# One fewer pick matmul per group, group rows in two halves, and scan flags in one PSUM buffer

## What is computed

```
def rgcn_conv(x, src, dst, edge_type, W, root, bias):      # second network, two layers (r0, r1)
    x_src = x[src]
    msg = sum over r of where(edge_type == r, x_src @ W[r], 0)
    norm = 1 / max(count of (dst, edge_type), 1)
    return segment_sum(msg * norm, dst) + x @ root + bias

def _nnconv(x, src, dst, edge_attr, ew, eb, rw, rb):       # fourth network, three layers (c0, c1, c2)
    W = (edge_attr @ ew + eb).reshape(E, 16, 16)
    msg = einsum('ei,eio->eo', x[src], W)
    return segment_sum(msg, dst) + x @ rw + rb
```

## Time and profile before

| | us |
|---|---|
| median of the runs | 12,188.94 |
| the profiled execution, its own time | 12,082.95 |
| its span, first to last instruction | 12,081.0 |
| TensorE matmuls busy | 9,816.9 |
| VectorE busy | 9,313.9 |
| ScalarE busy | 8,267.0 |
| GpSimd busy | 7,589.7 |

### The profile page before, as it was taken

One profiled execution on the slowest core, in us unless ns is written; L12 is line 12 of the kernel. 1 busy time (PEld: TensorE's weight loads), 2 busy tenths in 40 slices (PEclk: granted clock), 3 DMA queues, 4 the chain that ended last, 5 costly groups with the idle time before them and its releaser, 6 DMA issues. The chain is left out here.

```text
span 12081.0 us, 167867 instructions
## 1 busy us (share of the span) xinstructions
PE 9816.9 (81%) x42305; PEld 6821.8 (56%) x42305; DVE 9313.9 (77%) x14722; ACT 8267.0 (68%) x16314; POOL 7589.7 (63%) x6233
## 2 busy tenths in 40 slices
PE   5888888888885079878997688888899689969996
PEld 2333333333332057766775578777777577757775
DVE  7999999999997877764554699997666567656665
ACT  4777777777775057755775488885677467746774
POOL 4555555555556368876776677773677567756775
PEclk7666666666666589988998799998999799979997
DMA  3444444444444267765775111111888578858884
GB/s 117 178 178 177 176 177 178 178 178 178 178 176 138 91 244 269 260 229 188 249 248 167 50 46 44 45 45 26 276 287 290 182 260 293 284 183 268 287 289 161
DMA packets 750362, 2256.05 MB, mean 187 GB/s; under 512 B 272537, under 2 KB 420654, under 8 KB 673806
## 3 DMA queue, kind: packets, MB, share of 16 engines
q10 hardware_dynamic: 161280, 1027.68, 24.1%
q1 hardware_dynamic: 388638, 984.49, 21.7%
q0 software_dynamic: 200304, 242.20, 9.0%
HBM read 1321.84 MB, written 931.93 MB: 187 GB/s over the span
## 5 line engine op out<-in xcount | busy, mean ns | idle before, releaser
L592 POOL DMA_INDIRECT h<-in_x,idx x1568 | 2022.0, 1290 | 1731.9 <-DMA efT<-in_edge_attr_t 1269.9
L676 ACT ACTIVATE PX<-PX,h 128x16 f32<-128x16 f32 x12544 | 2510.5, 293 | 10.2 <-issue 3.8
L625 PE MATMUL PS<-M,minus_ident 128*128 128x512 f32 x1568 | 1417.5, 1030 | 313.9 <-DVE M L710 313.4
L1997 PE MATMUL PS<-mhr,lhs 128*128 128x392 f32 x6272 | 1262.6, 357 | 197.2 <-DVE lhs L2161 171.4
L1479 PE MATMUL PS<-every_weight,dstf 112*128 112x144 f32 (+1 forms) x8960 | 1273.8, 285 | 161.5 <-DVE dstf L1611 114.3
L1479 PEld LDWEIGHTS PS<-every_weight,dstf 112*128 112x128 f32 x8960 | 1223.3, 192 | 317.3 <-DVE dstf L1611 145.3
L1964 POOL DMA_INDIRECT myg<-node_table,mix x784 | 1103.7, 1408 | 447.7 <-issue 230.7
L2060 ACT ACTIVATE mhr<-mhb 128x1568 fp32r<-128x1568 bf16 x784 | 1142.1, 1505 | 294.6 <-DVE mhb L2151 239.0
L1997 PEld LDWEIGHTS PS<-mhr,lhs 128*128 128x128 f32 x6272 | 1152.5, 194 | 282.1 <-ACT mhr L2060 143.8
L613 PE MATMUL PS<-waug,efT 17*128 17x256 f32 x6272 | 1042.3, 535 | 300.0 <-DVE e L688 257.5
L613 PEld LDWEIGHTS PS<-waug,efT 17*128 17x128 f32 x6272 | 612.8, 252 | 1034.4 <-issue 495.6
(11 more groups left out here) (419 smaller groups left out, 20434.1 us busy)
## 6 DMA issues: line engine op xcount, KB each, us to landing
softmax_maxima<-M SPq DMA_DIRECT2D x196, 1024.0 KB
softmax_denominators<-ST SPq DMA_DIRECT2D x196, 1024.0 KB
softmax_numerators<-ST SPq DMA_DIRECT2D x196, 1024.0 KB
one_hot_rows_of_sources<-r0hb ACTq DMA_DIRECT2D x224, 896.0 KB
r1hb<-one_hot_rows_of_sources ACTq DMA_DIRECT2D x224, 896.0 KB
c0hb<-one_hot_rows_of_sources ACTq DMA_DIRECT2D x224, 896.0 KB
c1hb<-one_hot_rows_of_sources ACTq DMA_DIRECT2D x224, 896.0 KB
c2hb<-one_hot_rows_of_sources ACTq DMA_DIRECT2D x224, 896.0 KB
```

The costliest lines, as they stand in the source:

```text
L592: PO.indirect_dma_start(h[b.k][:, at(q), :], None, io["x"], bass.IndirectOffsetOnAxis(ap=idx[b.k][:, q:q + 1], axis=0))\
L625: mm = PE.matmul(PS[0:CH, 4 + n, :], minus[:, :], M[b.k % 2][:, n::4, :], start=False, stop=True)
L676: act = S.activation(PX[b.k][:, 1, t, D * i:D * i + D], PX[b.k][:, 0, t, D * i:D * i + D], ACT.Copy, scale=h[b.k][:, t, i:i + 1])
L1997: mm = PE.matmul(PS[:, 6 + k, 0:A7 // 2], lhs[(G * b.k + q) % 2][:, 2 * two + r, part, :], hr[(2 * G * b.k + j) % 4][:, r, k * A7 // 2:(k ...
```

## The change

It makes these edits:

- The nodes are split in 8 groups of 768 (`A8`, `KB` = 6 slices of 128 places) and a rest of 128 nodes, which counts as a seventh slice of group 0 (high part) and group 4 (low part). A group of edges takes 12 picks of 128 stationary columns and one of 80 columns (`last_parts`): 13.
- The group number is kept twice, once for partitions 0 to 63 and once for 64 to 127: `pick_a` has two halves, and the load of `ra` reads both, each broadcast to 64 partitions. The set-up computes, transposes and stores three arrays in place of two.
- Mask and weighing run over 128 partitions in place of 112.
- The flags `kp` of the scan lie in PSUM banks 2 and 3, one buffer for both blocks, and ScalarE waits for the scan of the block before in place of the second before.

```diff
-A9, KT = 7, 7
+A8, KB, KT = 8, 6, 7
+ROWS = 128 * KB
...
-        pick_a = dram("pick_a", (T, 128), I16)
-        pick_b = dram("pick_b", (T, 128), I16)
+        pick_a = dram("pick_group", (2, T, 128), I16)
+        pick_b = dram("pick_place", (T, 128), I16)
...
-            for n, d_ in enumerate((pick_a, pick_b)):
+            for n, d_ in enumerate((pick_a[0, :, :], pick_a[1, :, :], pick_b)):
...
-            V.tensor_scalar(pab[0][:, :], pab[1][:, :], float(128 * KT), None, ALU.is_ge).then_inc(*vd.up())
-            for k in range(2, A9):
+            V.tensor_scalar(pab[0][:, :], pab[2][:, :], float(ROWS), None, ALU.is_ge).then_inc(*vd.up())
+            V.tensor_scalar(pab[1][:, :], pab[2][:, :], float(A8 * ROWS), None, ALU.is_ge).then_inc(*vd.up())
+            for k in range(2, A8):
...
-            V.scalar_tensor_tensor(out=pab[1][:, :], in0=pab[0][:, :], scalar=-128.0 * KT, in1=pab[1][:, :],
+            V.scalar_tensor_tensor(out=pab[2][:, :], in0=pab[0][:, :], scalar=-float(ROWS), in1=pab[2][:, :],
+                                   op0=ALU.mult, op1=ALU.add).then_inc(*vd.up())
+            V.wait_ge(*vd.now())
+            V.scalar_tensor_tensor(out=pab[0][:, :], in0=pab[1][:, :], scalar=-float(A8 - 1), in1=pab[0][:, :],
+                                   op0=ALU.mult, op1=ALU.add).then_inc(*vd.up())
+            V.wait_ge(*vd.now())
+            V.scalar_tensor_tensor(out=pab[1][:, :], in0=pab[1][:, :], scalar=float(A8 // 2), in1=pab[0][:, :],
                                    op0=ALU.mult, op1=ALU.add).then_inc(*v2t.up())
             V.wait_ge(*pT_up.now())
-            V.wait_ge(*t2v.next(2 * NT))
+            turned_of = t2v.taken
             for k in range(NT):
-                for n in TWO:
+                for n in range(3):
+                    if 3 * k + n in (0, 32):
+                        V.wait_ge(t2v.sem, turned_of + min(3 * k + n + 32, 3 * NT))
                     V.tensor_copy(pT[0:wd[k], k, n, 0:CH], spread_at(k, n)).then_inc(*pT_up.up())
...
+            if c == KB:
+                big_, src_ = tn[:, A8 * KB, :], x[:, A8 * KB, :]
+                V.tensor_copy(last_parts[:, 0:D], big_).then_inc(*vd.up())
+                V.tensor_tensor(last_parts[:, 64:64 + D], src_, big_, ALU.subtract).then_inc(*vd.up())
+                return
...
+        PICKS = 2 * KB + 1
+        LOWEST = 6
...
-                    kp.append(sb(f"{name}kp{k}", [CH, D, TBC], F32, L))
+                    kp.append(PS[0:CH, 2:4, :].rearrange("p b c -> p (b c)")[:, 0:D * TBC].rearrange("p (f t) -> p f t", f=D))
...
-            mx = [dstf[0:A9 * D, 512 * k:512 * k + 512] for k in range(1 + LAG)]
+            mx = [dstf[:, 512 * k:512 * k + 512] for k in range(1 + LAG)]
...
-                SP.dma_start(ra[half][:, :], rows(b, half, pick_a)).then_inc(h_ra[half].sem, 16)
+                groups_of = pick_a[:, some(b, NG + 16 * half, 16), :].rearrange("h t c -> h (t c)")
+                SP.dma_start(ra[half][:, :], bc(groups_of, 64, 1)).then_inc(h_ra[half].sem, 16)
...
-                        mm = PE.matmul(PS[0:A9 * D, 4 + q % 2, :], parts[:, m % 2, m // 2, :],
-                                       hot_[q % 2][:, m // 2, :], start=(m == 0), stop=(m == 2 * KT - 1))
-                    if m0 < m1 == 2 * KT:
+                        if m == LOWEST:
+                            PE.matmul(PS[0:64 + D, 4 + q % 2, :], last_parts[:, :], hot_[q % 2][:, KB, :], start=False, stop=False)
+                            continue
+                        n = m - (m > LOWEST)
+                        mm = PE.matmul(PS[:, 4 + q % 2, :], parts[:, n % 2, n // 2, :],
+                                       hot_[q % 2][:, n // 2, :], start=(m == 0), stop=(m == PICKS - 1))
+                    if m0 < m1 == PICKS:
                         mm.then_inc(h_g.sem, 1)
...
-                    at = 2 * KT if both else 9
+                    at = PICKS if both else 9
...
-                    if due(n := b.on(-2).count(1, 1)):
+                    if due(n := b.on(-1).count(1, 1)):
                         S.wait_ge(*c_run.at(n))
```

More of the change, by code:

```diff
@@ L219, in program @@
         si = sb("srci", [CH, T], I32, setup)
-        pab = [sb(f"pab{k}", [CH, T], F32, setup) for k in TWO]
+        pab = [sb(f"pab{k}", [CH, T], F32, setup) for k in range(3)]
         NT = (T + 127) // 128
-        pT = sb("pT", [128, NT, 2, 128], I16, setup)
+        pT = sb("pT", [128, NT, 3, 128], I16, setup)
         wd = [min(128, T - 128 * k) for k in range(NT)]
@@ L237, in spread_at @@
         def spread_at(k, n):
-            return PS[0:wd[k], (2 * k + n) // 4, 128 * ((2 * k + n) % 4):128 * ((2 * k + n) % 4) + CH]
+            at = (3 * k + n) % 32
+            return PS[0:wd[k], at // 4, 128 * (at % 4):128 * (at % 4) + CH]
         def setup_sync():
@@ L398, in setup_tensor @@
             for k in range(NT):
-                for n in TWO:
+                for n in range(3):
+                    if 3 * k + n == 32:
+                        PE.wait_ge(pT_up.sem, 1 + 32)
                     PE.transpose(spread_at(k, n), pab[n][:, 128 * k:128 * k + wd[k]], ident[0:CH, 0:CH])\
                         .then_inc(*t2v.up())
-            PE.wait_ge(*pT_up.next(2 * NT + 1))
+            PE.wait_ge(*pT_up.next(3 * NT + 1))
         setup_sync()
@@ L1200, in program @@
         node_of = [dstf[:, PG * k:PG * k + PG] for k in range(3)]
-        parts = sb("parts", [128, 2, KT, A9 * D], F32R)
+        parts = sb("parts", [128, 2, KB, A8 * D], F32R)
+        last_parts = sb("parts_of_last_rows", [128, 64 + D], F32R)
         pick = sb("pick", [128, KT], F32)
@@ L1227, in conv_constants_vector @@
             V.tensor_reduce(pick_row[:, :], gi[:, :], X, ALU.add).then_inc(*vd.up())
+            V.tensor_scalar(last_parts[:, :], ones[:, 0:64 + D], 0.0, None, ALU.mult).then_inc(*vd.up())
         conv_constants_pool()
@@ L1493, in steps @@
                         if nx:
-                            pick_rows(nx, q, at, 2 * KT)
+                            pick_rows(nx, q, at, PICKS)
                 def first(b):
@@ L1610, in mask @@
                         V.wait_ge(*h_sel.at(n))
-                    V.scalar_tensor_tensor(out=mx[q % (1 + LAG)][:, :], in0=ra[q // 4][0:A9 * D, 512 * (q % 4):512 * (q % 4) + 512],
-                                           scalar=pick_row[0:A9 * D, 0:1], in1=PS[0:A9 * D, 4 + q % 2, :],
+                    V.scalar_tensor_tensor(out=mx[q % (1 + LAG)][:, :], in0=ra[q // 4][:, 512 * (q % 4):512 * (q % 4) + 512],
+                                           scalar=pick_row[:, 0:1], in1=PS[:, 4 + q % 2, :],
                                            op0=ALU.is_equal, op1=ALU.mult).then_inc(h_mk.sem, 1)
@@ L1808, in whole @@
                     V.memset(run[k][:, :, :], 0.0).then_inc(*vd.up())
-                    V.memset(kp[k][:, :, 0:1], 0.0).then_inc(*vd.up())
+                V.memset(kp[0][:, :, 0:1], 0.0).then_inc(*vd.up())
                 V.wait_ge(*vd.now())
```

17 lines of the change are left out of this document (9 added, 8 removed).

## The result

| | before | after |
|---|---|---|
| median of four runs each, timed side by side | 12,183.69 us | 13,277.56 us |
| ratio, with its 95% interval | | 1.0901 (1.0888 to 1.0914) |
| profiled execution, its own time | 12,082.95 us | 13,286.02 us |
| its span | 12,081.0 us | 13,284.8 us |

The forecast was 13,033 us with a range of 12,740 to 13,500. By medians the change costs 1,094 us; by the two profiled executions 1,204 us, because the profiled execution of before was 0.8% faster than this median and that of after was not.

The account below looks back on a forecast made before the run. TensorE was taken to set the pace, GpSimd close behind. Stages of 6,129 us less the present 5,300 gave +829, set-up +15, flags 0, the picks' gain lost in waiting; on the 12,189 median, 13,033 us, range 12,740 to 13,500.

Parts of the forecast that it names:

- The step that decides: Load of group rows: a source with outermost dimension 2 uses two DMA engines, whose throughput sets the blocks; +829 us.
- The signs named for it: Trace after: 130 packets a load, mask's wait longest in all stages (5 to 10 us), DMA share towards 0.7, lower clock.
- The term that was short: Convolution stages: 43.4 (r0), 40.8 (r1) and 44.9 us (c) a block, 6,129 us in all against the present 5,300.
- the plateau's: DMA price taken from a plateau of 426 GB/s in the trace: 26.6 for one engine, before 5% for lacking work.
- The dear end: Hot engine priced by c1's busy shares: 51.2 us a block in c, about 47 in r1 and 52 in r0.
- Outside the stages: Set-up before the barrier: more operations, transposes, copies and stores cost +15 us, bounds 10 to 20.
- The picks: TensorE: one of 14 picks goes, 0.238 us a group, 267 us in all; 128 columns cost nothing; gain goes into waiting.
- The flags: Scan flags in PSUM: put at 0; at most 140 us gained through GpSimd, of use in r0 alone.
- rival (d): Scan slows on PSUM: to double, 284 us more, 12,278 us in a spread-out kernel; chance 0.02.
- (a): Load of group rows spread over all sixteen engines or changing pairs, TensorE's pitch counts: 11,994 us (11,930 to 12,110); chance 0.10.
- (b): Same two hot DMA engines but dearer, under about 24 GB/s each: +1,788 us, 13,977 us; chance 0.05.
- (c): Two DMA engines hot, but present slack swallows most, needing over 28 GB/s each: about 12,200 to 12,750 us; chance 0.03.

Follow-up runs that it names:

- e1: The kernel after with each load of group rows made as two loads of 64 partitions; 11,212.57 us, 0.9636 of before on a fast chip.
- e2: The kernel before with its group table stored twice and loaded with an outermost dimension of 2; 13,046.75 us, 1.1211 of before on a fast chip.
- e6: The kernel after with four buffers of group rows and each load issued a block earlier; 13,078.87 us, 1.1239 of before on a fast chip.
- e8: The kernel before with 13 picks of 112 columns, the low part of the last slice left out; 11,623.20 us, 0.9994 on a fast chip.
- e10: The kernel before with 13 picks of 112 columns and the scan flags in PSUM, one buffer; 12,150.20 us, 0.9994 on a slow chip.
- e11: The kernel before with 13 picks of 112 columns and group rows loaded as two loads of 64 partitions; 12,160.88 us, 0.9995 on a slow chip.
- e5: The kernel before with only the scan flags moved to PSUM, one buffer; 11,491.64 us, 0.9879 of before on a fast chip.
- e4: The kernel after with two loads of 64 partitions and the flags back in two SBUF buffers; 11,303.35 us, 0.9715 of before on a fast chip.
- e12: The kernel after with two loads of 64 partitions per load of group rows, run on a slow chip; 12,086.74 us, 0.9938 of before.
- e9: The kernel before, unchanged, run again for its trace on a slow chip; 12,185.21 us in one run.

## Why the prediction was right, and where not

**The step that decides held.** The 13,278 us lie inside the range, and by the mechanism that was forecast. The forecast rested on one claim, that a source with an outermost dimension of 2 is moved by two engines, read off the 18 completions of 6,250 pieces. E1 and e2 show it from both sides, the packet counts number for number: 130 in place of 144 a load. The signs named for it came for the most part: the mask's wait VectorE's longest in c (10 us each, up to 15.5; I had said 5 to 10) and in r0 (only 3.9 us each), but second in r1 (221 us, where VectorE's waits for the weighing sum to 248); a DMA share of 0.69 (0.7), 221 GB/s in c (235), the lower clock behind a wait. "The lead hides latency, not throughput" is e6.

**The term that was short.** The stages were put at 43.4, 40.8 and 44.9 us a block (r0, r1, c); they took 42.1, 44.1 and 47.6. All 28 blocks of each are 6,412 us for the 6,129 forecast, 283 us short; 35 more come from the stretches of before, which I had cut 35 us wider than from first pick to last (5,300 for 5,265). The bytes of the hot engine, 1,137,408 in c, over 47.6 us are 23.9 GB/s, r1's 1,032,960 over 44.1 are 23.4, r0's 26.1; my price was 26.6 less 5%, 25.3. From the packets of the trace of after in c1: 128 of 4 KB at a median of 0.165 us, 64 of 7 KB at 0.273, 24 of 4,608 bytes at 0.205 (0.159, 0.272 and 0.178 before) and 1.8 us of small ones make 45.3 us, so the engine worked 95% of the time, as I had chosen, and its price a byte was 6% above the plateau's (an estimate from medians, since the trace names no engine). I had let the waiting in the mean shares fall away with fourteen engines idle. It did not: the one-hot queue's packets took 0.459 x 1,347 x 16 = 9,892 us in c1, and 9,302 before. The plateau of the earlier trace rows comes from another load; in this mixed stream a byte cost more. R1, which has the fewest bytes, came out dearer than r0. Why, I can't say. The dear end (47 to 52 us a block, 21 to 22 GB/s) lay beyond all three. One sum of mine is off by 4 us: 28 x (41.3 + 38.8 + 3 x 42.8) - 5,300 + 15 is +553, a low end of 12,742.

The sum fell short by more than the time shows. Between the profiled executions, to which it was fitted, 1,204 us were lost for the 844 forecast; by medians it was 1,094, and the 13,033 us, set on the median, missed by 245. That it came so near is in part luck.

**Outside the stages** I had +15 us. The barrier is left 12.7 us later, for the earlier trace rows:

```profile
49.33 1.79 DVE L382 SCALAR_TENSOR_TENSOR pab<-pab 128x1568 f32<-128x1568 f32 x1
51.16 1.79 DVE L385 SCALAR_TENSOR_TENSOR pab<-pab 128x1568 f32<-128x1568 f32 x1
62.26 6.43 DVE L399 CAST pT<-PS 128x128 int16<-128x128 f32 x32 [5.67 <-PE PS L414]
70.54 1.46 DVE L399 CAST pT<-PS 128x128 int16<-128x128 f32 x7 [1.85 <-PE PS L414]
78.15 0.23 DVE L529 TENSOR_SCALAR minus_ident<-ident 128x128 f32<-128x128 f32 x1 [6.14 <-PEq L422]
```

The order was as worked out, with two-operand passes of 1.79 for 1.82 us and a barrier left at 78 for 80. Another 40 us outside the stages have no term in my sum; by medians the whole change was 1,094, so part of them may belong to the one fast execution of before.

**The picks.** 0.238 us each off TensorE was nearly right: narrow groups stand 4.21 us apart with 14 picks and 3.98 with 13 (e8), wide ones with 13 stand 4.02 apart. The width costs at most 0.003 us a pick, inside my bounds. That TensorE sets the pace of the kernel before was not shown by the rows I read, and on the fast kind e8 speaks against it. I had read a line of work without gaps and called it the bound, with GpSimd "close behind". I counted 0.27 us between two gathers, the part put down to issue; in the trace of before the gap is 0.305 us in the median and never under 0.303. That makes GpSimd's least time 672 x (1.150 + 0.305) = 978 us of c1's 1,052, and 672 x (1.276 + 0.305) = 1,062 of r0's 1,067, where next to no slack is left. On the fast kind no gather of e8 waits in any of the five stages, so GpSimd is the bound in all, and a pick less was worth nothing; on the slow kind a pick less was worth nothing either (e10, e11).

**The flags.** Put at 0 with 140 as the most, "of use in r0 alone": on the fast kind they gave 139 us alone (e5) and some 91 on top of the mended load (e1 against e4), in r0 and c. The step that failed is the place, since c was taken to have slack on GpSimd. That 139 meets 140 is luck: I had up to 1 us a block in all 140 blocks, and from e8 to e5 r0 gains 1.5, c 0.9 to 1.0 and r1 none. The Trainium skill, "SBUF — State Buffer", section "Who interferes with whom", has the rule: an instruction with two SBUF inputs contends with a GpSimd instruction that reads SBUF, one with a single input, outside VectorE's two-port modes, doesn't. The scans agree (2.15 against 0.94 us). The page infers that the generation of descriptors is not touched by two-input products; the gathers, which read their indices from SBUF, are (0.54 and 0.31 us in e8), and the measurement decides. The one-hot rows with their single input, which stretch r0's gathers by 0.95 us, would fall under the exception; no run shows in which mode they run. I weighed the rule and let the row speak against it, but the row only showed where gathers were longest, not where they mattered. That ScalarE's copy would wait for nothing new held: no such wait is listed in e5. The scan takes 2,024 ns for the earlier trace rows 2,026, so rival (d) is out.

**The rivals.** (a), the load spread out, is what e1 and e12 make true by hand. I had 11,994, 195 us under before, by 47 us saved in a c stage. Measured: 0.9938 (e12) on the kind of chip that the case ran on, some 80 us (about 12,108 on its 12,184, just inside the 11,930 to 12,110 that I gave), with c stages only 12 to 23 us under e9's; and 425 us on the fast kind. TensorE's pitch fell as said, but the pitch was not what held the stages. (b) and (c) fall with the stages' 47.6 us.

**The version that beats both** is e1's: the change as it is, with two loads of 64 partitions in place of one. It takes 0.9636 of before's time on the fast kind and 0.9938 on the slow.

## What to carry to other kernels

Before a load's access pattern is given a new outermost dimension, ask how many engines can share it, and count its packets before and after: a small number ahead of the broadcast can cost more than any matmul that it saves, and two plain loads in its place cost nothing that showed. Add busy and idle time of each engine in a stage: one whose gaps are all of the same length (here 0.305 us) is the bound, or level with it as in e1, however short of 100% its busy share looks. An edit that frees the lower of two close limits is worth nothing alone (e8), and one that frees the higher gains no more than the distance between them; test such edits in pairs.

## What the runs showed of the hardware that I had not expected

- A scan (2.02 us) with both operands in SBUF holds up a gather that starts inside it, 2.15 for 0.94 us; with one operand in PSUM it takes the same 2.02 us and costs the gather nothing. On the fast kind that was 1.2% of the kernel (e5).
- The same kernel before takes 11,631 us on one chip and 12,184 in the case's measurement, 4.8% more. Between the profiles of e8 (which takes the time of before) and e9, 436 of 577 us lie in the convolution stages (c1 975 and 1,059 us), as stalls between instructions, not as slower instructions: a gather is 1,155 and 1,156 ns. An edit's worth on one kind says little about the other, unless it is as large as the two hot DMA engines: 1.0901 on the slow kind for the change, 1.1211 on the fast for its load alone.
